# Step tables of 16-bit instead of 32-bit words in a graph kernel: three convolutions and two attention layers

## The reference, cut to what matters

```python
# L0, for each of 3 hops
h = h * out_norm[:, None]
h = segment_sum(h[src], dst, num_segments=N) * in_norm[:, None]
h = h @ W[i] + b[i]                      # relu between hops
# L1, for each of 2 layers (self loops are added to the edges)
h = (x @ W).reshape(n, 4, 64)
alpha = leaky_relu(a_src[src] + a_dst[dst])
e = exp(alpha - segment_max(alpha, dst)[dst])
out = segment_sum(e / segment_sum(e, dst)[dst] * h[src], dst) + bias
```

## Time and profile before

| | us |
|---|---|
| median of 3 runs | 6783.42 |
| lowest, highest | 6779.98, 6793.79 |
| span of the profiled execution | 5649.0 |
| own time of the profiled execution | not given |
| three convolution stages, first to last gather's start | 162.3 to 1140.7, 1210.9 to 2188.4, 2259.7 to 3237.3 |
| two attention stages, first to last gather's start | 3314.8 to 4361.8, 4478.0 to 5527.6 |
| busy: PE, DVE, ACT, POOL | 4218.4, 3705.7, 2101.0, 4159.4 |

### The profile page before, as it was taken

One profiled execution on the slowest core, in us unless ns is written; L12 is line 12 of the kernel. 1 busy time (PEld: TensorE's weight loads), 2 busy tenths in 40 slices (PEclk: granted clock), 3 DMA queues, 4 the chain that ended last, 5 costly groups with the idle time before them and its releaser, 6 DMA issues.

```text
span 5649.0 us, 84292 instructions
## 1 busy us (share of the span) xinstructions
PE 4218.4 (75%) x14997; PEld 2470.4 (44%) x14997; DVE 3705.7 (66%) x12168; ACT 2101.0 (37%) x7038; POOL 4159.4 (74%) x4290
## 2 busy tenths in 40 slices
PE   8677777777777778677777777777777677777772
PEld 7433333343333335333333355555554455555551
DVE  7555555555555554555555568777777677777777
ACT  4000000020000003000000088888887688888881
POOL 8677777777777777777777747777776677777776
PEclk7777677787777668777777778878888888888886
DMA  2443333333333333433333354444444344444444
GB/s 94 117 111 106 106 105 106 105 108 106 106 105 105 105 106 100 131 105 105 106 106 106 106 167 110 110 110 110 110 111 125 99 110 110 110 110 110 110 112 151
DMA packets 309459, 625.61 MB, mean 111 GB/s; under 512 B 85044, under 2 KB 180264, under 8 KB 308937
## 3 DMA queue, kind: packets, MB, share of 16 engines
q0 software_dynamic: 192928, 530.18, 33.3%
q1 hardware_dynamic: 109656, 88.65, 5.0%
q10 hardware_dynamic: 6384, 1.39, 0.1%
HBM read 573.37 MB, written 47.33 MB: 110 GB/s over the span
## 4 chain that ended last, share of the span: by engine, by line
PE 40%; POOL 20%; DMA 14%; issue 11%; DVE 10%; ACT 5%; POOLq 0%; DVEq 0%; SPq 0%; ACTq 0%
PE main L1071 20%; POOL ring L667 13%; PE main L1174 11%; DMA ring<-conv_tab,csrc 9%; DMA ring<-attn_tab,sidx 5%; POOL ring L679 5%; DVE acc L1365 3%; PE main L990 3%; POOL ring L699 2%; PE pso L1094 2%; ACT ring L912 2%; DVE ring L1226 1%; ACT oh L890 1%; DVE ad L1584 1%; PE pso L982 1%
## 5 line engine op out<-in xcount | busy, mean ns | idle before, releaser
L667 POOL DMA_INDIRECT ring<-conv_tab,csrc x2346 | 2222.6, 947 | 749.2 <-issue 590.4
L1071 PE MATMUL main<-ring,oh 128*128 x4992 | 2207.0, 565 | 758.2 <-DVE acc L1365 325.1
L1365 DVE TENSOR_TENSOR acc<-acc,main 128x264 f32 (+2 forms) x4160 | 1761.8, 424 | 1254.2 <-PE main L1071 1157.6
L679 POOL DMA_INDIRECT ring<-attn_tab,sidx x1664 | 1590.8, 956 | 604.5 <-issue 361.7
L1071 PEld LDWEIGHTS main<-ring,oh 128*128 128x128 f32 x4992 | 1092.0, 259 | 1869.7 <-issue 1801.3
L1174 PE MATMUL main<-ring,oh 128*128 128x264 f32 x3328 | 1246.2, 491 | 120.6 <-ACT ring L912 69.2
L912 ACT ACTIVATE ring<-ring 128x64 f32<-128x64 f32 x3328 | 910.9, 343 | 0.0
L1357 DVE TENSOR_SCALAR oh<-iota,dloc 128x128 f32<-128x128 f32 x2505 | 814.8, 325 | 91.9 <-issue 79.6
L1174 PEld LDWEIGHTS main<-ring,oh 128*128 128x128 f32 x3328 | 619.3, 229 | 290.3 <-DVE ring L1690 222.8
L890 ACT ACTIVATE oh<-iota,dloc 128x128 f32<-128x128 f32 x1664 | 528.9, 394 | 3.4 <-DMA attn_tab<-oh 3.4
L1690 DVE TENSOR_TENSOR ring<-ring 128x128 f32<-128x128 f32 x1664 | 463.1, 284 | 0.0
(11 more groups left out here) (212 smaller groups left out, 2993.3 us busy)
## 6 DMA issues: line engine op xcount, KB each, us to landing
ring<-conv_tab,csrc POOLq DMA_INDIRECT x2346, 2.7
ring<-attn_tab,sidx POOLq DMA_INDIRECT x1664
ring<-attn_tab SPq DMA_DIRECT2D x14, 896.0 KB, 8.5
conv_tab<-oh SPq DMA_DIRECT2D x12, 896.0 KB, 4.0
flag_room<-start_rows SPq DMA_DIRECT2D x416, 8.0 KB
flag_room<-end_rows SPq DMA_DIRECT2D x416, 8.0 KB
x_tab<-acc SPq DMA_DIRECT2D x7, 896.0 KB
oh<-x_tab SPq DMA_DIRECT2D x7, 896.0 KB
```

Source lines behind the costliest of these rows:

```text
L667: pool.indirect_dma_start(ring3[:, c % U, 0:C], None, conv_tab[k], bass.IndirectOffsetOnAxis(ap=csrc[:, c:c + 1], axis=0)).then_inc(gather ...
L679: pool.indirect_dma_start(ring3[:, j, 0:TW], None, attn_tab[l], bass.IndirectOffsetOnAxis(ap=sidx[:, i * GB * G + j:i * GB * G + j + 1], a ...
L1071: nc.tensor.matmul(main[s % 4][:, 0:width], oh[:, (s % OHR) * P:(s % OHR + 1) * P], ring[:, bass.ds(slots[s % 8], width)], start=True, sto ...
L1365: nc.vector.tensor_tensor(a, a, main[k][:, 0:width], ALU.add).then_inc(added, 1)
```

## The change

The four tables hold 16-bit unsigned words: the rows that VectorE casts to, the copy in device memory and the table in SBUF. A row of `step_tab` has still 896 words and now 1792 bytes, so that 8 words take 16 bytes and 16 words take 32. `step_values` and its callers stay as they are; the loads are still one instruction for 8 or 16 registers.

```diff
+U16 = mybir.dt.uint16
...
-        step_words = dram("step_words", (4, SX), I32)
+        step_words = dram("step_words", (4, SX), U16)
...
-        step_tab = flag_room[H * G:H * G + 4, 0:SX].bitcast(I32)
+        step_tab = flag_room[H * G:H * G + 4, 0:SX // 2].bitcast(U16)
...
-        step_rowsT = oh[0:4 * SB, o_k + 3 * SX:o_k + 3 * SX + P].bitcast(I32)
+        step_rowsT = oh[0:4 * SB, o_k + 3 * SX:o_k + 3 * SX + P // 2].bitcast(U16)
```

## The result

The changed kernel takes 6910.2 us (median of 4 runs, 6902.2 to 6916.1), the kernel before beside it 6782.6 us (4 runs, 6780.0 to 6793.8): ratio 1.0184, 95% interval 1.0169 to 1.0198, so 128 us or 1.8% slower. The forecast was 6782.6 us with a range from 6768 to 6900.

The account below looks back on a forecast made before the run. GpSimd's gathers, one every 1.25 us, were taken as the bound, hiding the loads in gather stages. The attention tails gave 0.51 + 0.25 = 0.8 us, so 6783.4 - 0.8 = 6782.6 us, range 6768 to 6900 us.

Parts of the forecast that it names:

- the upper bounds of 2.07 and 4.14: Table loads: us for 8 and 16 narrow words if they lose what makes a row quick.
- the slow rival: Table loads on TensorE and VectorE go word by word: 0 to 385 us slower, middle 6975 us; chance 0.22.
- The rival's sum for eight steps: TensorE's convolution steps plus two slow loads, 9.2 or 10.6 us, against 9.42 us that the gathers take.
- good case: Convolution steps at VectorE's backlog pace of 0.63 us: eight need 9.2 us with slow loads, and nothing is lost.
- bad case: Convolution steps at TensorE's 0.874 us: eight need 10.6 us with slow loads, 1.2 us too much, times 312 = 360 us.
- the rival's point of decision: Price per 8-word load from which slow loads cost time: about 2.2 us at best, about 1.5 us at worst.
- the 1134 us between the two: Profiled span of 5649.0 us against the runs' median of 6783.42 us; the difference was claimed to lie outside the span.
- the third rival: TensorE bounds the kernel after all, so shorter loads save up to 214 us: 6570 us, or 6680 with half; chance 0.10.
- The tails' term: After the last gathers of the attention stages, shorter VectorE loads give back 0.51 + 0.25 = 0.8 us.
- The tables' build: VectorE's cast and small transfers before the first table load: halved bytes are hidden by 119 us, no effect.

Follow-up runs that it names:

- the wider load: 16-bit kernel with a `max` on arrival counts, TensorE loading 16 counts per eight convolution steps and using eight: 6190.8 us, against 5655.5 us without the extra words.
- the pairs with few stalls: 32-bit and 16-bit kernels, both with 484 TensorE and 293 GpSimd stalls added in the convolutions: 7169.8 and 7453.8 us; repeated, 7178.8 and 7464.4 us.
- the three pairs of quiet twins: 32-bit against 16-bit tables, both with a `max` on arrival counts: 5647.4 and 5655.5 us, 5647.7 and 5657.1 us, 5647.1 and 5655.6 us.
- the doubled loads: Changed kernel with TensorE's convolution table loads issued twice in the source; the trace has no more loads than without the edit: 5655.8 us, ratio 1.0006.
- the first pair of stalls: 32-bit and 16-bit kernels with empty instructions before drawn TensorE steps and GpSimd gathers, which did not stay in the program: 5647.7 and 5657.1 us.

## Why the prediction was wrong

Two steps failed: the price of a narrow load, and the reading that the timed executions run like the profiled one.

**The price of a load** was mis-sized: the step was "if the cost goes by bytes, 8 half-words cost 0.075 + 0.515 / 2 = 0.33 us". They cost 1.92 us, 16 cost 3.79, near the upper bounds of 2.07 and 4.14 that the slow rival used. The slope between 8 and 16 words was read from rows of 32-bit words and carried to rows of another kind, of which the trace had none. The load of 4 aligned 32-bit words, 0.33 us, shows that the sum was sound for bytes that are read as words. It also contradicts the floor of about 600 ns that the Trainium skill gives in "DMA: Bandwidth & Descriptors", "Latency and other measured facts". The other rule weighed, some 200 ns a register even in bulk ("Runtime: NRT & Kernel Launch", "Instruction fetch mechanics", of the Trainium skill), is stated for loads from device memory; it is near the 234 ns measured here for narrow or shifted words in SBUF, and 3.1 times the 64 ns of aligned 32-bit ones.

**What hides it.** "GpSimd, which waits for neither, keeps its 1.25 us" is right for a quiet job even with loads 1.3 us longer in place of 0.26 shorter: 5655 against 5652 us. The rival's sum for eight steps was 9.2 us of 9.42 in its good case and 10.6 in its bad one; the wider load puts TensorE 0.15 us below the pace of the gathers, so by this estimate the rival's point of decision (2.2 us a load, or 1.5) lies at 1.92 + 0.15 / 2 = 2.0 us. The changed kernel stands just short of it.

**The step that decided** was "the 1134 us between the two lie outside its span", with "The change touches nothing that the trace places there". They are inside the span. Every execution of the kernel before in the later jobs has a span 1.8 to 1.9 us under its time, at 5650 us and at 6780 us alike (6773.2 for 6775.0 us, for one), so the execution that was profiled was a quiet one and the timed ones were disturbed. With queues held up for 0.7 us hundreds of times, GpSimd did not keep its 1.25 us: the first stage's gathers took 1143 us in place of 978. By the estimate above TensorE's 2.8 us of room can absorb far more of such stops than its 0.15 us. The condition that was timed was thus another than the one from which the room was read; the third rival had this reading ("if it runs otherwise than the profiled one"), with the opposite sign because it believed in shorter loads. The slow rival came nearest, with 0 to 385 us and a middle of 6975 us, but not by its own mechanism alone: at 1.92 us a load its bad case gives 8 x 0.874 + 3.84 - 0.57 - 9.42 = 0.84 us in eight steps, 260 us in all, at the pace of the quiet trace, where 3 us were measured. That the 128 us fell inside its bounds is in part luck.

**Where the 128 us go.** Shown: the long loads are hidden in quiet jobs, a further 1.87 us on TensorE is not, and 16 bits cost 284 to 338 us in disturbed jobs with stalls added and 128 without. Some 28 to 54 us of the cost stand in the attention part, which leaves 74 to 100 for the convolutions, by estimate. Not shown: a stage by stage account of the 128 us, since no disturbed trace of 32-bit tables without stalls exists; the convolutions' share is a difference, not a measurement. Two things stand beside the story of TensorE's room. No run lengthened VectorE's loads alone, while TensorE's largest named wait in the trace after is for VectorE's one-hots (761 us); which queue's loads cost how much is open. And the granted clock is lower where the tables are narrow and the job disturbed: 0.71 for the changed kernel, 0.72 to 0.73 for before in another such job, 0.69 against 0.71 in the pairs with few stalls. In quiet jobs it is the other way round, 0.79 against 0.77. Whether the lower clock is a part of the cost or comes of the waiting was not separated.

**The small terms.** The tails' term had the right place and the wrong sign. From the last gather of each attention stage to the next gather or the end it is 116.2 and 121.4 us before, and 119.1 and 125.0 us in the quiet trace of the changed kernel; in the three pairs of quiet twins the 16-bit kernel's two tails are 4 to 8 us longer together. The loads in them got longer by 2.5 us each, where the prediction had them give back 0.8 us in all. That is the size of the quiet difference of 3 us (8 to 9 between the twins). The tables' build can't be seen: the first gather starts at 162.3 us in both quiet traces.

**Open:** what holds up the queues. It came on the same chip that was quiet in another job, and it is there with either width. The page's instruction and data queues move the same bytes in both conditions.

## What to carry to other kernels

Before counting on a narrower table, read one load of exactly that kind: width, alignment and count set its price, and full aligned 32-bit words are 3.6 times cheaper each. When a profiled span lies far under the timed median, suspect that the timed runs are stretched inside, and ask what room each engine has beside the bound: here an edit that used up the room of the other engines was free in a quiet profile and was paid for when the queues were interrupted. An experiment that adds work must be seen in its trace; three here (the doubled loads and the first pair of stalls) added nothing.

## What the runs showed of the hardware

- A load into registers took about 64 ns a word from aligned 32-bit rows (0.33, 0.59, 1.10 us for 4, 8, 16 words) and 234 ns a word from 16-bit rows or from 32-bit rows shifted by four bytes (1.92 to 1.93 us for 8, 3.79 to 3.80 for 16), a little less on VectorE (1.83, 3.59).
- In disturbed jobs single instructions of 17 to 51 ns on TensorE's, GpSimd's and SyncE's queues took about 0.7 us, sometimes twice that (1.40 us). VectorE's register operations stayed at 71 ns or less and ScalarE's semaphore instructions at 38 ns or less. Of GpSimd's 15,888 semaphore instructions in the 32-bit kernel with few stalls, 11,720 of them added, 1032 were hit.
- In such a job 484 added stalls on TensorE and 293 on GpSimd, 320 and 199 us by design, made the 32-bit kernel 389 us slower (7170 for 6781), about twice what GpSimd's alone would be. That longer queues are hit more often may explain it; no run separates it.
- The kernel with 32-bit tables and a `max` on the arrival counts was 5 to 7 us faster than before in three quiet jobs (each 0.999, upper bounds 0.9999 to 1.0). That is 0.1%; why was not tried.
